# First units of a post-norm transformer layer: warm products, v by weight blocks, another order of splits and sums

## What is computed

```python
q = rope((x @ Wq.T + bq).reshape(B, S, H, D)); k = rope((x @ Wk.T + bk)...); v = (x @ Wv.T + bv)...
qk = einsum('bshd,bstd->bsht', q, k) / sqrt(D)         # heads against heads, H = 16, D = 32
att = softmax(qk, axis=-1)
out = swapaxes(einsum('bsht,bstd->bshd', att, v), 1, 2).reshape(B, S, E) @ Wo.T + bo
x = layernorm(x + out)
g, u = (x @ gate_w.T) * gate_s, (x @ up_w.T) * up_s
x = layernorm(x + ((silu(g) * u) @ down_w.T) * down_s)
```

## Time and profile before

| | us |
|---|---|
| median of 3 runs | 1682.94 |
| lowest and highest run | 1681.45, 1684.80 |
| the profiled execution | 1683.66 |
| its span, first to last instruction | 1681.9 |
| TensorE busy | 1651.6 (98%) |
| VectorE busy | 1312.3 (78%) |
| ScalarE busy | 981.4 (58%) |
| GpSimd busy | 629.3 (37%) |

### The profile page before, as it was taken

The page is one execution under the profiler, slowest core; times in us unless marked ns, Lnnn a source line. Parts: engine busy times, 40 slices in busy tenths (PEclk is TensorE's granted clock), DMA queues, the critical chain, the costliest instruction groups (busy, mean ns, idle before and its releaser), DMA issues.

```text
span 1681.9 us, 40839 instructions
## 1 busy us (share of the span) xinstructions
PE 1651.6 (98%) x14958; PEld 1355.2 (81%) x14958; DVE 1312.3 (78%) x1932; ACT 981.4 (58%) x1578; POOL 629.3 (37%) x690
## 2 busy tenths in 40 slices
PE   8899999999999999998999999999999999999997
PEld 6688888888888888886788888888888888888886
DVE  7789999999999999987667676676766766767656
ACT  5666666666666666656455554555545545556453
POOL 7767666676667666652101102011011020110112
PEclk9999999999999999999999999999999999999999
DMA  6678778787777778778843534535445355353351
GB/s 211 152 178 174 180 174 196 169 178 176 185 190 164 188 173 189 179 171 229 263 142 118 183 104 155 167 102 185 158 140 159 103 195 160 97 191 124 112 180 60
DMA packets 438708, 275.53 MB, mean 164 GB/s; under 512 B 257280, under 2 KB 377216, under 8 KB 438656
## 3 DMA queue, kind: packets, MB, share of 16 engines
q1 hardware_dynamic: 438512, 274.61, 60.2%
q10 hardware_dynamic: 144, 0.26, 0.0%
HBM read 181.74 MB, written 93.06 MB: 163 GB/s over the span
## 4 chain that ended last, share of the span: by engine, by line
PE 94%; DVE 2%; issue 1%; ACT 1%; SPq 0%; POOL 0%; DMA 0%; POOLq 0%; DVEq 0%; ACTq 0%
PE ps_x L636 13%; PE ps_x L640 13%; PE ps_x L637 12%; PE ps_s L891 9%; PE ps_s L896 9%; PE ps_x L891 7%; PE ps_x L896 7%; PE ps_x L902 5%; PE ps_x L906 5%; PE ps_s L780 3%; PE ps_a L767 3%; PE ps_a L902 2%; PE ps_a L906 2%; PE ps_s L902 2%; PE ps_s L906 2%
## 5 line engine op out<-in xcount | busy, mean ns | idle before, releaser
L891 PE MATMUL ps_s<-x_hi,slot 128*128 128x512 f32 x672 | 264.1, 393 | 0.5
L896 PE MATMUL ps_s<-x_lo,slot 128*128 128x512 f32 x672 | 261.7, 389 | 0.0
L1483 POOL TENSOR_TENSOR z<-z,xr 128x512 f32<-128x512 f32 x60 | 77.3, 1316 | 480.4 <-DVE z L1824 480.4
L891 PE MATMUL ps_x<-x_hi,slot 128*128 128x512 f32 x560 | 219.0, 391 | 1.3 <-ACT sg L1187 0.6
L896 PE MATMUL ps_x<-x_lo,slot 128*128 128x512 f32 x560 | 218.0, 389 | 0.0
L1074 ACT ACTIVATE kX<-kT 32x512 f32<-32x512 f32 x256 | 161.2, 630 | 66.2 <-DVE kT L1592 45.4
L1755 DVE TENSOR_TENSOR hid<-ps_s,hid 128x512 f32<-128x512 f32 x88 | 60.8, 690 | 122.7 <-ACT hid L1195 122.7
L891 PEld LDWEIGHTS ps_s<-x_hi,slot 128*128 128x128 f32 x672 | 126.1, 188 | 34.7 <-ACT u L1226 4.3
L896 PEld LDWEIGHTS ps_s<-x_lo,slot 128*128 128x128 f32 x672 | 126.2, 188 | 25.2
L902 PE MATMUL ps_x<-wd,h 128*128 128x512 f32 x352 | 137.1, 390 | 0.2 <-DVE h L1796 0.2
L906 PE MATMUL ps_x<-wd,h 128*128 128x512 f32 x352 | 137.0, 389 | 0.0
(11 more groups left out here) (176 smaller groups left out, 4395.4 us busy)
## 6 DMA issues: line engine op xcount, KB each, us to landing
slot<-gu_hi SPq DMA_DIRECT2D x88, 896.0 KB, 5.1
xc<-x_cols SPq DMA_DIRECT2D x32, 512.0 KB, 3.8
v_rows<-v_in SPq DMA_DIRECT2D x32, 512.0 KB, 2.8
v<-v_rows SPq DMA_DIRECT2D x32, 512.0 KB, 5.2
res<-x_rows SPq DMA_DIRECT2D x64, 256.0 KB, 3.8
x_rows<-x_out SPq DMA_DIRECT2D x32, 512.0 KB, 3.8
x_cols<-x_turn SPq DMA_DIRECT2D x128, 128.0 KB, 2.5
raw<-x_cols SPq DMA_DIRECT2D x64, 256.0 KB, 5.1
```

What stands on the lines that cost most here:

```text
L891: pe.matmul(out[:, :], slot[:, WEIGHTS[i], cols], x_hi[:, i, k], start=start, stop=False, skip_group_check=True)
L896: last = pe.matmul(out[:, :], slot[:, WEIGHTS[i], cols], x_lo[:, i, k], start=False, stop=stop, skip_group_check=True)
L1483: pool.tensor_tensor(z[:, h, r], z[:, h, r], rows_of_x1(n, h)[:, r], ALU.add).then_inc(z_added[h], 1)
```

## The change

It does this, all ahead of the loops:

- TensorE first multiplies ten times a 128x128 f32 block of zeroes (`warm`, the first eight rows of `prob`, set by one more memset on GpSimd), then makes v of unit 0 with the weight block k as the outer loop and both tiles inside, with one wait for each operand (`first_v`).
- x of unit 0 arrives in two transfers, one for each tile, with a semaphore each.
- The low parts of Wo move from GpSimd to VectorE, between `own4` and `subtract_top(0)`.
- On VectorE the split of Q5 moves behind unit 0's q, that of Q6 behind the first v bias of unit 1, that of Q7 behind unit 1; `turn_k(0, 1)` moves behind `turn_q(0, 0)`, `turn_prob(0)` behind the first q of unit 1.
- On ScalarE the high parts of Q5, Q6, Q7 and Q4 move later, those of tile 1 and of unit 2's tiles earlier, and `top_of_slab(0)` behind the sums of unit 2.
- On GpSimd the low parts of tile 1 come first, those of unit 2 and the first slab's sums earlier; `sums_of_slab(1)` moves behind the three `low_of_sum(2, ...)`.

The diff, cut to its core:

```diff
 OPENING = 4
+WARM = 10
 DIRECT = 2
...
             prob = sb("prob", [P, 2 * Q32, H], F32, early)
+            warm = prob[:, 0:8].rearrange("p n k -> p (n k)")
             with ExitStack() as staged:
...
         xc_loaded, xc1_loaded = sem("xc_loaded"), sem("xc1_loaded")
+        x0_loaded = [xc_loaded, sem("x0_second_loaded")]
         res_loaded = [sem(f"res_loaded{t}") for t in range(2)]
...
             load_weight(WV, 0)
-            sp.dma_start(x_view(xc), x_cols2[0]).then_inc(xc_loaded, 16)
+            for t in range(2):
+                sp.dma_start(x_view(xc)[:, t], x_cols2[0, :, t]).then_inc(x0_loaded[t], 16)
             for k in range(1, KE):
...
                 for k in range(KE):
-                    if isinstance(m, int) and m == 0:
-                        pe.wait_ge(wv_hi_done, k + 1)
-                        pe.wait_ge(wv_lo_done, k + 1)
                     last = three(ps_x[bank][:, :], hi[:, t, k], lo[:, t, k], wv_hi[:, k], wv_lo[:, k],
                                  k == 0, k == KE - 1, ahead if k == KE - 1 else None)
                 last.then_inc(v_done, 1)
+
+            def first_v():
+                for k in range(KE):
+                    for t in range(2):
+                        out = ps_x[BANK_Y if t else BANK_W][:, :]
+                        if t == 0:
+                            pe.wait_ge(wv_hi_done, k + 1)
+                        pe.wait_ge(a_hi_done, t + 1)
+                        pe.matmul(out, a_hi[:, t, k], wv_hi[:, k], start=k == 0, stop=False, skip_group_check=True)
+                        pe.wait_ge(wv_lo_done, k + 1)
+                        pe.matmul(out, a_hi[:, t, k], wv_lo[:, k], start=False, stop=False, skip_group_check=True)
+                        pe.wait_ge(a_lo_first, t + 1)
+                        last = pe.matmul(out, a_lo[:, t, k], wv_hi[:, k], start=False, stop=k == KE - 1, skip_group_check=True)
+                        if k == KE - 1:
+                            last.then_inc(v_done, 1)

...
             K_HALVES, Q_HALVES = (Q1, Q2), (PLAIN, Q3)
-            project_v(0, 0)
-            project_v(0, 1)
+            pe.wait_ge(power_set, 1)
+            for _ in range(WARM):
+                pe.matmul(ps_x[BANK_X][:, 0:P], warm, warm, start=True, stop=True)
+            first_v()
             plain_product(0, 0, K_HALVES, BANK_X)
...
                 elif isinstance(m, int) and m == 0:
-                    act.wait_ge(xc_loaded, 16)
+                    act.wait_ge(x0_loaded[t], 16)
                 else:
...
             high_of_block(Q3)
-            high_of_block(Q5)
             high_of_tile(1, 0)
             high_of_tile(1, 1)
             spread_k(0, 0)
-            high_of_block(Q6)
+            high_of_block(Q5)
             spread_k(0, 1)
             for k in range(KE):
                 high_of_wo(k)
+            high_of_block(Q6)
+            high_of_tile(2, 0)
+            high_of_tile(2, 1)
             high_of_block(Q7)
-            high_of_block(Q4)
             high_of_slab(0)
             exponent(0)
-            high_of_tile(2, 0)
-            high_of_tile(2, 1)
+            high_of_block(Q4)
             spread_k(1, 0)
-            top_of_slab(0)
             spread_p(0)
             spread_k(1, 1)
             high_of_sum(2, Q6)
             high_of_sum(2, Q7)
             high_of_sum(2, Q5)
+            top_of_slab(0)
             high_of_slab(1)
...
                         copy_s1(0, 0)
-                        act.wait_ge(power_set, 3)
+                        act.wait_ge(power_set, 4)
                         act.activation(table[:, :], ones[:, :], ACT.Silu)
...

+            pool.memset(warm, 0.0).then_inc(power_set, 1)
             pool.memset(power[:, :], -0.5).then_inc(power_set, 1)
             pool.memset(eps[:, :], EPS).then_inc(power_set, 1)
             pool.memset(ones[:, :], 1.0).then_inc(power_set, 1)
             pool.memset(kX[:, :, :, :, :], 0.0).then_inc(kX_zeroed, 1)
-            pool.wait_ge(power_set, 3)
-
-            def low_of_wo(k):
-                pool.wait_ge(wo_hi_done, k + 1)
-                pool.tensor_tensor(wo_lo[:, k], wvo_raw[:, k], wo_hi[:, k].bitcast(F32), ALU.subtract)\
-                    .then_inc(wo_lo_done, 1)
+            pool.wait_ge(power_set, 4)

...

+            low_of_tile(1, 0)
+            low_of_tile(1, 1)
             sum_of_weights(Q5)
             sum_of_weights(Q6)
-            low_of_tile(1, 0)
-            low_of_tile(1, 1)
+            sums_of_slab(0)
             sum_of_weights(Q7)
-            sum_of_weights(Q4)
-            sums_of_slab(0)
-            for k in range(KE):
-                low_of_wo(k)
-            low_of_slab(0)
-            sums_of_tiles(2)
             low_of_tile(2, 0)
             low_of_tile(2, 1)
-            sums_of_slab(1)
+            sum_of_weights(Q4)
+            sums_of_tiles(2)
+            low_of_slab(0)
             low_of_sum(2, Q6)
             low_of_sum(2, Q7)
             low_of_sum(2, Q5)
+            sums_of_slab(1)
             low_of_slab(1)
...
                    .then_inc(wv_lo_done, 1)
+
+            def low_of_wo(k):
+                dve.wait_ge(wo_hi_done, k + 1)
+                dve.tensor_tensor(wo_lo[:, k], wvo_raw[:, k], wo_hi[:, k].bitcast(F32), ALU.subtract)\
+                   .then_inc(wo_lo_done, 1)

...
             turn_k(0, 0)
-            low_of_block(Q5)
             plain_k(0, 1)
-            turn_k(0, 1)
             plain_q(0, 0)
             turn_q(0, 0)
+            turn_k(0, 1)
             plain_q(0, 1)
             turn_q(0, 1)
+            low_of_block(Q5)
+            add_v_bias(1, 0)
             low_of_block(Q6)
-            add_v_bias(1, 0)
+            add_v_bias(1, 1)
             dve.wait_ge(late_loaded, 16 * 3)
             dve.tensor_reduce(own4[:, :], ident[:, :].rearrange("p (r j k) -> p j r k", r=2, j=A4), AX.XY,
                               ALU.max).then_inc(own_made, 1)
+            for k in range(KE):
+                low_of_wo(k)
             subtract_top(0)
-            low_of_block(Q7)
-            add_v_bias(1, 1)
-            sums_of_prob(0)
             plain_k(1, 0)
             turn_k(1, 0)
+            sums_of_prob(0)
             scale_prob(0)
             plain_k(1, 1)
-            turn_prob(0)
             plain_q(1, 0)
             turn_q(1, 0)
+            turn_prob(0)
+            plain_q(1, 1)
             turn_k(1, 1)
-            plain_q(1, 1)
             turn_q(1, 1)
+            low_of_block(Q7)
             low_of_block(Q4)
```

## The result

The kernel after takes 1690.44 us (median of 6 runs, 1687.70 to 1691.13), the kernel before 1683.80 beside it (6 runs, 1681.45 to 1684.80): the ratio is 1.0036, with a 95% interval of 1.0026 to 1.0047. It is slower by more than 0.2%. The forecast was 1688.0 within 1679.5 to 1691.5, with slower as the likeliest side. So side and range held. The median lies 2.4 us above the forecast, and as will be seen the last link of the argument was wrong, so that the close hit is in part luck.

The account below looks back on a forecast made before the run. The bound was the slab chain: VectorE, ScalarE, GpSimd's low_of_slab(1), SyncE's store and load, to unit 3's kX product. Span 1681.9 plus 5.1 is 1687.0; as execution 1688.7, median 0.7 lower: 1688.0, range 1679.5 to 1691.5.

Parts of the forecast that it names:

- Opening: Unit 0 start: zero products, v by weight blocks, x in two transfers bring the key product to 11.75, 3.1 us ahead.
- The splits of Wo: VectorE's four low_of_wo take turns with GpSimd: 7.4 us from 30.6, ending 38.05, so subtract_top(0) comes 4.8 us later.
- Rival 1: VectorE keeps its turn between the low_of_wo splits, which end at 33.7: +0.8, 1683.8 us; chance 22%.
- Down the chain to `low_of_slab(1)`: From subtract_top(0) over ScalarE and GpSimd, with sums_of_slab(1) behind low_of_sum(2, ...): low_of_slab(1) ends at 60.2, before 55.2, +5.1 us.
- Neither adds: both end before the slab chain does: TensorE's waits at unit 2, 5 us at its start and some 3 ahead of Q7, cost nothing extra.
- SyncE's queue keeps its length: SyncE's store and load behind low_of_slab(1) take as long as before, so the product at 74.24 comes at 79.3.
- The clock at 0: No loss counted for TensorE's clock falling in the new waits of 5 and 3 us at unit 2.
- rival 4: Clock falls in TensorE's new waits of 5 and 3 us, slow in the bursts: +3 us more, 1691; chance 6%.
- The stall at 0: TensorE's 3.6 us issue stall behind the kX wait moves along unchanged: 0, bounds -4.9 to +1.5 us.
- Rival 3: TensorE's issue stall falls away while it waits for kX: +5.1 - 4.9, 1683.1 us; chance 7%.
- Rival 2: Opening pays: TensorE's queue sets the end, 5.9 us gained, 1677.0, if low_of_slab(1) ends before 54.4, subtract_top(0) near 30.5; 17%.
- Adding up: Whole sum: only the later end of low_of_slab(1) counts, +5.1 us, putting the product behind the kX wait at 79.3.

Follow-up runs that it names:

- the opening alone: Kernel before plus only the products of zeroes, v by weight blocks and x in two transfers, all orders as before: 1684.76 us, ratio 1.0004.
- GpSimd stands: Kernel after plus one wait: GpSimd holds before low_of_tile(2, 0) until VectorE's four splits of Wo are done: 1687.06 us, ratio 1.0019.
- the slab's sums first: Kernel after with sums_of_slab(1) moved back ahead of the three low_of_sum(2, ...) on GpSimd: 1687.00 us, ratio 1.0014.

## Why the prediction held, and where it was wrong

**Opening: right.** Zero products from 1.00 (foreseen 1.0) to 5.2 (5.3), the key product at 12.06 (11.75, before 14.82), and no gain at the end. The run with the opening alone shows the last directly.

**The splits of Wo: right.** They started at 31.43 (30.6) and took 6.65 us (7.4 to 38.05); `subtract_top(0)` came at 38.00. The start was 0.8 us later and the length 0.8 shorter, so part of the hit is luck. The mechanism is not: 2.48 us when GpSimd stands, and single ends at 32.43, 34.12, 36.93 and 38.08, where 31.75, 33.65, 36.7 and 38.05 were foreseen. Rival 1 falls with it.

**Down the chain to `low_of_slab(1)`: right.** `turn_prob(0)` ended at 48.19 (48.2), ScalarE's high parts of the sums began at 53.33 (53.3), `low_of_slab(1)` ended at 60.32 (60.2), and the new place of `sums_of_slab(1)` cost 2.23 us of wait on ScalarE.

**"Neither adds: both end before the slab chain does": wrong.** This is the step that failed. The prediction saw both waits of TensorE (4.2 and 2.2 us, foreseen 5 and 3) and put them aside, because SyncE's chain was to end at 79.3. It ended at 77.93. "SyncE's queue keeps its length" failed by 1.2 us: from `low_of_slab(1)` to `load_slab(2)` were 3.32 us before (55.20 to 58.52) and 2.09 after, because one store's issue that had taken 1.68 us took 0.43. The first row is from the kernel before, the second from the kernel after:

```profile
55.59 1.68 SPq L440 DMA_DIRECT2D gu_hi<-f_hi  x1
```

```profile
60.71 0.43 SPq L444 DMA_DIRECT2D gu_hi<-f_hi  x1
```

Meanwhile TensorE's own path came to 79.61: the later Q7 and twelve products at the lower clock. The softmax chain over VectorE won the race by 1.7 us. Both paths grow from the same late `high_of_slab(1)`, and they lay so close (79.3 foreseen for one, 79.6 measured on the other) that the wrong one gave nearly the right number. That is luck. The prediction had named the sign itself: no wait for `kX` at unit 3 would show that the slab chain doesn't set the end.

**The clock at 0: too low, by 1.6 us.** This is rival 4, given 6%. Its clock loss came, behind the 2.17 us wait; what it held against itself, the slack of 1.7 us, was the slack of a path that no longer set the end. Of the two waits that it named only the second counted: the fall of the clock behind the first cost 2.4 us of products and was hidden by the wait ahead of Q7. Its 1691 is nearer to the 1690.4 than the forecast is.

**The stall at 0: within its bounds.** 4.43 against 3.63 us, +0.8, inside -4.9 to +1.5. (Its lower bound was added up wrongly: 0.39 x 2 in the window and as much ahead are 1.6 us, not 1.3, which would make it -5.2; nothing else rests on it.) Rival 3 has nothing for it: the stall was there in all fourteen kernels, with 0 or 5.0 us of wait ahead of the burst. What ends it stays open; its length doesn't follow AV(1) in the table, and it was 3.22 us behind the wait of 5.0 and 4.43 behind none.

**Rival 2: it did not come, and its condition was never met in full.** With Wo off VectorE's critical place the maximum did come at 31.2 to 31.9, but `low_of_slab(1)` ended at 55.4 us or later in all twelve kernels, never before 54.4 as the rival asked: GpSimd's load and the store of slab 0, which the rival left out, became the next limits. What a kernel with both halves of the condition would take stays open.

**Adding up: +5.1 foreseen, +5.3 at AV(1).** The 5.3 consist of 4.6 for Q7, 1.6 for the clock and -0.8 for the wait for `kX`; the slab chain, from which the +5.1 came, moved by 3.8 (74.09 to 77.93).

## What to carry to other kernels

When two chains end within a microsecond or two of each other, work out both to the same instruction and say how much the second has in hand; a wait may be put aside only by a chain whose own length has been checked part by part, issues of DMAs included. An instruction moved from GpSimd to VectorE doesn't cost its own length if both then work in SBUF: price it by what GpSimd has queued in that stretch. And where one edit moves a loss without shrinking it, look for the buffer that a store still reads: in five of these kernels a transfer's landing held ScalarE, and behind it the softmax, with the compute in five different orders.

## What the runs showed of the hardware

- VectorE's subtraction of two SBUF operands, four in a row, 128x512 each: 2.48 us with GpSimd standing, 6.65 beside GpSimd's splits and sums; copies of the same size beside it 5.58. The turn passes on between consecutive instructions of one engine (each split ended 0.55 us behind one GpSimd instruction), so a run of short instructions keeps no right of way.
- A wait added on GpSimd gave time back: 4.36 us of standing, 3.4 us off the median.
- The granted clock was at 0.50 from 66.0 to 68.0 us in the kernel after, behind one wait of 2.17 us with full work before and after. In the kernel with the slab's sums first the wait was 0.35 and this fall didn't come; nor did it in the kernel before behind waits of 1.55 and 0.60 us (1.00 from 44 to 50 us).
- Ten 128x128 products of zeroes before the first data end the slow start: 0.23 us a product instead of 0.43, worth 2.4 us at the key product, while the granted clock read 1.00 in the first 14 us with and without them.
- TensorE's stall inside the burst of small products behind unit 1 took 3.19 to 5.15 us in these fourteen kernels. Its cause is open.
- The store `gu_hi` of slab 0, 308 KB, took 4.3 to 6.2 us from issue to landing in the fourteen kernels, with loads and another three stores issued beside it; that of slab 1 took 2.8 us at 60.71 in the kernel after. Its issue on SyncE took 0.43 us in most cases, 1.68 and 1.64 in two (the kernel before and the one with the opening alone).
